# The experts' first product with its weights stationary and its tokens moving

## The reference, cut to what matters

```
t = rmsnorm(layernorm(h), norm_scale)
g = t @ gate_w.T + gate_b                       # 16 experts
top_vals, top_idx = top_k(g, 4); route_w = softmax(top_vals)
h1 = einsum('nh,ech->nec', t, mlp1_w) + mlp1_b  # per expert 192 -> 768
a  = min(glu, 7) * sigmoid(1.702 * min(glu, 7)) * (clip(lin, -7, 7) + 1)
y  = einsum('nec,ehc->neh', a, mlp2_w) + mlp2_b # per expert 384 -> 192
out = x + sum over experts of comb[n, e] * y[n, e]
```

## Time and profile before

| | |
|---|---|
| median of 3 runs | 792.63 us (792.56 to 793.79) |
| the profiled execution | 790.85 us, its span 789.1 us |
| PE busy | 695.0 us (88% of the span), 4250 instructions |
| PEld (weight loads) | 416.3 us (53%) |
| DVE, ACT, POOL busy | 434.6 (55%), 389.8 (49%), 347.8 us (44%) |
| mean granted clock of TensorE | 0.942 of full speed |
| DMA | 76.60 MB, mean 97 GB/s |

### The profile page before, as it was taken

How to read it: one execution, slowest core, us unless ns; L and a number is a source line. 1 busy time by engine, 2 the same in 40 slices (tenths; PEclk the granted TensorE clock), 3 DMA queues, 4 the chain that set the end, 5 groups by cost and what they waited for, 6 DMA issues and landing times.

```text
span 789.1 us, 15394 instructions
## 1 busy us (share of the span) xinstructions
PE 695.0 (88%) x4250; PEld 416.3 (53%) x4251; DVE 434.6 (55%) x1275; ACT 389.8 (49%) x784; POOL 347.8 (44%) x403
## 2 busy tenths in 40 slices
PE   4588989788867999999999995699999999999990
PEld 4557786578632222222222223377777777777760
DVE  0153757675672577777666644355555555555540
ACT  0032436533313999899989891134434344343430
POOL 4121223222230255555555444156666666666661
PEclk9798999999995999999999996599999999999995
DMA  9999980000014122322222200233323333233324
GB/s 275 411 389 320 321 274 1 1 1 1 21 55 108 61 55 104 98 91 100 63 82 103 103 24 22 79 68 52 52 43 51 52 52 52 43 51 52 52 31 70
DMA packets 31140, 76.60 MB, mean 97 GB/s; under 512 B 4335, under 2 KB 24672, under 8 KB 28672
## 3 DMA queue, kind: packets, MB, share of 16 engines
q1 hardware_dynamic: 17156, 59.50, 24.1%
q0 software_dynamic: 12400, 15.50, 9.8%
q10 hardware_dynamic: 1552, 1.18, 0.5%
HBM read 59.49 MB, written 40.11 MB: 126 GB/s over the span
## 4 chain that ended last, share of the span: by engine, by line
PE 72%; DVE 9%; DMA 4%; POOL 4%; ACT 4%; issue 3%; SPq 1%; ACTq 0%; DVEq 0%; POOLq 0%
PE ps L815 13%; PE ps L946 11%; PE ps L947 11%; PE ps L802 9%; PE ps L965 8%; PE ps L656 3%; DMA big<-patches 3%; PE ps L956 3%; ACT mid L1073 2%; POOL rstd L443 2%; PE ps L732 1%; DVE stat L1165 1%; DVE mid L1173 1%; PE ps L742 1%; PE ps L629 1%
## 5 line engine op out<-in xcount | busy, mean ns | idle before, releaser
L1073 ACT ACTIVATE mid<-ps 128x1536 f32<-128x1536 f32 x144 | 200.1, 1457 | 27.1 <-PE ps L802 27.1
L815 PE MATMUL ps<-mid 128*32 128x384 f32 x1152 | 123.6, 502 | 3.4 <-POOL mid L491 2.0
L566 POOL TENSOR_TENSOR mid<-mid 128x384 f32<-128x384 f32 x63 | 62.5, 991 | 99.8 <-PE ps L956 78.0
L946 PE MATMUL ps<-big,mid 128*128 x252 | 104.6, 497 | 0.3 <-issue 0.3
L947 PE MATMUL ps<-big,mid 65*128 x252 | 104.0, 493 | 0.0
L802 PE MATMUL ps<-mid 52*128 52x512 f16 x432 | 88.3, 389 | 6.2 <-ACT mid L1073 5.6
L965 PEld LDWEIGHTS ps<-big,mid 128*128 128x128 f32 x378 | 64.6, 189 | 18.4 <-issue 2.0
L965 PE MATMUL ps<-big,mid 128*128 x378 | 71.9, 326 | 1.5 <-DVE mid L1509 1.5
L1501 DVE TENSOR_SCALAR mid<-ps 128x384 f32<-128x384 f32 x63 | 35.1, 558 | 68.6 <-PE ps L947 68.6
L517 POOL DMA_INDIRECT expert_in<-t_row,slot_u x48 | 47.9, 999 | 46.0 <-DVE slot_u L1391 35.0
L1115 ACT ACTIVATE mid<-ps,mid 128x192 f32<-128x192 f32 x63 | 26.6, 422 | 84.3 <-PE ps L965 81.4
(11 more groups left out here) (224 smaller groups left out, 1192.7 us busy)
## 6 DMA issues: line engine op xcount, KB each, us to landing
expert_in<-expert_in SPq DMA_DIRECT2D x16, 1358.5 KB, 36.4
mid<-expert_in SPq DMA_DIRECT2D x63, 104.5 KB, 2.1
big<-patches SPq DMA_DIRECT2D x3, 2048.0 KB, 32.0
big<-w_a SPq DMA_DIRECT2D x4, 1536.0 KB
big<-w SPq DMA_DIRECT2D x4, 1152.0 KB
big<-w_b SPq DMA_DIRECT2D x4, 780.0 KB
big<-patches SPq DMA_DIRECT2D x4, 512.0 KB, 7.5
expert_in<-zero_rows POOLq DMA_DIRECT2D x1, 1567.5 KB, 16.2
```

The costliest lines, as they stand in the source:

```text
L566: nc.gpsimd.tensor_tensor(actv[r], prod[r], sig[r], ALU.mult).then_inc(actv_ready, 1)
L815: last = nc.tensor.matmul(oacc[32 * g:32 * g + 32, 0:QW], vhead[par][:, kb, :], probs[kb % 3][:, g * QW:(g + 1) * QW], start=(kb == 0), st ...
L946: nc.tensor.matmul(o, xtT[r][:, 0:P], w1a_sb[:, bass.ds(ex * 768 + half * FF, FF)], start=True, stop=False)
L1073: nc.scalar.activation(probs[kb % 3], SETS[kb % 2], ACT.Exp, scale=0.5).then_inc(probs_ready, 1)
```

## The change

The first weights are no longer kept in SBUF. SP fetches them for every tile, four tiles deep (NW = 4): `w1_t[q]` (128 rows by 768) and, as two transfers, `w1_h[q]`, in which rows 128 to 191 of the glu half lie at partitions 0 to 63 and those of the lin half at partitions 64 to 127. In the product the weights are stationary, in pieces of 128 columns, and the 128 transposed tokens move. The result is then already transposed (expert channels on partitions), so `act_transpose` and `actT_copy` are gone, and `mlp2` takes `actv` as it is. The products with 64 rows use the two row groups of the array through `tile_position`; for that, channels 128 to 191 of each token must lie on both partition halves, so `t_row` carries them twice (RW = 273) and the second token transpose is full. The bias is a column per expert and piece, `b1_cols`, made once: a transfer of 96 rows of 128, a transpose on TensorE before the first head, and two DVE operations. DVE adds it in `clip`, in pieces of 128 columns; the +1 of lin is in its bias. SP issues the weights of tiles 0 and 1 after `plan_ready` and ahead of its wait for `rows_out`. `mlp2` has two banks, 5 and 6. ACT's `sigmoid` and `y_tile` and POOL's `expert` and `add_rows` do the same work as before.

```diff
-COMB = C
-TOKEN = C + E
-RW = C + E + 1
+COMB = C + CB
+TOKEN = COMB + E
+RW = TOKEN + 1
+NW = 4
+HROW = P // 2
...
-        w1a_sb = big[:, 0:E * 768]
-        w1b_sb = big[:, E * 768:2 * E * 768]
-        w2_sb = big[:, 2 * E * 768:]
+        at[0] = 0
+        v_perm = carve(NT * C).rearrange("p (t c) -> p t c", t=NT)
+        w2_sb = carve(E * 3 * C)
+        w1_t = [carve(768) for _ in range(NW)]
+        w1_h = [carve(FF) for _ in range(NW)]
+        b1_rows = carve(P)[0:E * 6]
+        b1_cols = carve(E * 6)
+        t_row = carve(RW)
...
+            sp.wait_ge(v_in, 16 * NB)
+            sp.dma_start(b1_rows, w1_b[CB:CB + 1, :].rearrange("o (k c) -> (o k) c", c=P)).then_inc(b1_in, 16)
             for e in range(0, E, 4):
-                loads += [(w1b_sb[0:CB + 1, e * 768:(e + 4) * 768], w1_b[:, e * 768:(e + 4) * 768]),
-                          (w2_sb[:, e * 3 * C:(e + 4) * 3 * C], w2[:, e * 3 * C:(e + 4) * 3 * C]),
-                          (w1a_sb[:, e * 768:(e + 4) * 768], w1_a[:, e * 768:(e + 4) * 768])]
...
+                sp.wait_ge(vhead_ready, e // 4 + 1)
+                sp.dma_start(w2_sb[:, e * 3 * C:(e + 4) * 3 * C], w2[:, e * 3 * C:(e + 4) * 3 * C]).then_inc(w_in, 16)
...
+            def load_weights(j, q):
+
+                if not isinstance(j, int) or j >= NW:
+                    sp.wait_ge(h_done, j * 2 - (2 * NW - 2))
+                ex = sp.value_load(ej_i[0:1, bass.ds(j, 1)], min_val=0, max_val=E - 1)
+                sp.dma_start(w1_t[q], w1_a[:, bass.ds(ex * 768, 768)]).then_inc(w1_in[q], 16)
+                for half in range(2):
+                    sp.dma_start(w1_h[q][HROW * half:HROW * half + CB, :],
+                                 w1_b[0:CB, bass.ds(ex * 768 + half * FF, FF)]).then_inc(w1_in[q], 16)
...
+            load_weights(0, 0)
+            load_weights(1, 1)
+            sp.wait_ge(rows_out, 16 * (TOPK * NT + 1))
+            load_rows(0, 0)
+            load_rows(1, 1)
...
+            with sp.Fori(1, MT // NW) as i:
+                for q in range(NW):
+                    load_weights(i * NW + q, q)
+                    load_rows(i * NW + q, q % 2)
...
-                    pool.wait_ge(aT_psum, j - 1)
+                    pool.wait_ge(y_psum, j - 1)
...
+            pe.wait_ge(b1_in, 16)
+            nc.tensor.transpose(b7[:, 0:E * 6], b1_rows, ident[0:E * 6, 0:E * 6]).then_inc(b1_psum, 1)
             pe_head(0, None, 0, True, False)
...
-                nc.tensor.transpose(o[0:CB, P:2 * P], xt[r][:, P:C], ident[:]).then_inc(x_read, 1)
+                nc.tensor.transpose(o[:, P:2 * P], xt[r][:, P:2 * P], ident[:]).then_inc(x_read, 1)
+
+            def mlp1(j, q, n_loaded):
+
+                r = q % 2
+                pe.wait_ge(xT_ready, j + 1)
+                pe.wait_ge(w1_in[q], n_loaded)
+                if not isinstance(j, int) or j >= 2:
+                    pe.wait_ge(lin_ready, j - 1)
+                banks = [bank(1 + 2 * half + r) for half in range(2)]
+                for half in range(2):
+                    for c in range(3):
+                        nc.tensor.matmul(banks[half][:, c * P:(c + 1) * P], w1_t[q][:, half * FF + c * P:half * FF + (c + 1) * P],
+                                         xtT[r][:, 0:P], start=(c == 0), stop=False)
+                for c in range(3):
+                    for half in range(2):
+                        rows_ = slice(HROW * half, HROW * half + CB)
+                        last = nc.tensor.matmul(banks[half][:, c * P:(c + 1) * P], w1_h[q][rows_, c * P:(c + 1) * P],
+                                                xtT[r][rows_, P:2 * P], start=False, stop=(c == 2),
+                                                tile_position=(HROW * half, 0))
+                        if c == 2:
+                            last.then_inc(h_done, 1)
...
                 pe.wait_ge(actv_ready, j + 1)
+                if not isinstance(j, int) or j >= 2:
+                    pe.wait_ge(y_sb, j - 1)
                 for c in range(3):
...
+                    last = nc.tensor.matmul(bank(5 + r)[:, 0:C], actv[r][:, c * P:(c + 1) * P],
...
+            def tile_work(j, q, loaded):
+
+                if not isinstance(j, int) or j + 1 < MT:
+                    x_transpose(j + 1, (q + 1) % 2, loaded * 2 + 16 * ((q + 1) // 2 + 1))
+                mlp1(j, q, loaded * 3 + 48)
+                if not isinstance(j, int) or j >= 2:
+                    mlp2(j - 2, q % 2)
...
-                nc.scalar.activation(xtT[r][:, 0:P], o[:, 0:P], ACT.Identity)
-                nc.scalar.activation(xtT[r][0:CB, P:2 * P], o[0:CB, P:2 * P], ACT.Identity).then_inc(xT_ready, 1)
+                nc.scalar.activation(xtT[r], o[:, 0:2 * P], ACT.Identity).then_inc(xT_ready, 1)
...
+                nc.vector.scalar_tensor_tensor(t_row[:, C:C + CB], ln[:, P:C], rms[:], nscale_sb[:, P:C], ALU.mult, ALU.mult)
...
+                ex = dve.value_load(ej_i[0:1, bass.ds(j, 1)], min_val=0, max_val=E - 1)
...
+                for c in range(3):
+                    last = nc.vector.tensor_scalar(glu[r][:, c * P:(c + 1) * P], bank(1 + r)[:, c * P:(c + 1) * P],
+                                                   b1_cols[:, bass.ds(ex * 6 + c, 1)], 7.0, ALU.add, ALU.min)
+                last.then_inc(glu_ready, 1)
...
+                for c in range(3):
+                    last = nc.vector.tensor_scalar(lin[r][:, c * P:(c + 1) * P], bank(3 + r)[:, c * P:(c + 1) * P],
+                                                   b1_cols[:, bass.ds(ex * 6 + (3 + c), 1)], 8.0, ALU.add, ALU.min)
+                last.then_inc(lin_ready, 1)
```

139 lines of the change are left out of this document (37 added, 102 removed).

## The result

The changed kernel takes **788.69 us** (median of 4 runs, 788.33 to 788.94) against 793.21 us before (4 runs beside them): ratio 0.9942, 95% interval 0.9925 to 0.9959. So it is faster by 0.6%, some 4.5 us, where I had forecast 770. The profiled execution has a span of 787.1 us.

The account below looks back on a forecast made before the run. TensorE was taken to bound the expert stage: 4.11 to 3.67 us a tile, counted 62 times, gives -27.3 us. With +4.6 once per run, the profiled 790.85 became 768.2; placed 1.8 below the median, this gave 770 us, range 755 to 804.

Parts of the forecast that it names:

- SyncE at 3.5 us a tile: Expert stage: SyncE's work per tile with the added weight transfers, 3.5 us, just under TensorE's 3.67; bounds 3.3 and 3.9.
- a fuller queue: SyncE in the expert stage: a transfer's issue might rise from 0.34 to 0.45 us, making 3.9 us a tile.
- rival (B): Expert stage: SyncE is the bound at 3.9 us a tile, 784 us in all; chance 0.15.
- TensorE's side: Expert stage: TensorE's work per tile falls from 4.11 to 3.67 us and sets the tile, -27.3 us.
- The borders: First product on TensorE: entering and leaving the row-tiled part costs 0.46 us a tile; lower bound nothing.
- Rival (A): First product: the row groups do not overlap, half part 1.34 us, tile 4.34 us, 811 us in all; chance 0.24.
- DMA bytes: Expert stage: the DMA engines need 2.85 us a tile, below 3.67, a share of 0.78.
- Rival (C): Expert stage: scattered rows land later, POOL and ACT wait, tile 4.0 us, 790 us in all; chance 0.07.
- the opening's larger zero rows: Opening transfer: zero rows grow by 31%, 480 KB, costing +1.2 us; bounds 0 and 3.0.
- The bias wait: Before the attention: TensorE's transpose of b1 waits for its transfer, delaying L815 by 2.7 us; bounds 1.5 and 3.5.
- SyncE's start: After the plan: SyncE issues six weight transfers before the first token rows, +1.7 us; bounds 0 and 3.
- The tail: End of the last tile: no activation transposes and no copy of them, -1.0 us.

Follow-up runs that it names:

- e18_before: The kernel before, unchanged, profiled once more: 792.97 us.
- e19_after: The changed kernel, unchanged, profiled once more: 789.23 us.
- e1_fixed: The changed kernel with first-product weights fetched for the first four tiles only and reused by all later tiles: 766.49 us.
- e6_serial: Against e1_fixed, both 64-row halves of the first product set on row group 0, reading the first half's weights: 806.48 us.

## Why the prediction failed

By the second pair of profiles (e18_before and e19_after; both with long heads), the difference is made up so, all from first or last starts of instructions. Each is one execution, and the parts ahead of the plan vary by 1 to 3 us between executions of one program:

| part | forecast | measured |
|---|---|---|
| first weighted sum (L815, L834) | +3.9 | 249.67 to 253.33: +3.7 |
| from there to the plan | 0 | 250.2 to 249.4: -0.7 |
| plan to first product | +1.7 | 7.3 to 10.3: +3.0 |
| first product to the last second product's start | -27.3 | 263.4 to 251.8: -11.6 |
| from there to the end | -1.0 | 20.7 to 22.6: +1.9 |
| span | -22.7 | 791.2 to 787.5: -3.7 |

**The step that failed: SyncE at 3.5 us a tile.** The sum was 1.39 for the work it had, 1.23 for three transfers with what lies around them, 0.57 for a register load and 0.3 for gaps. Measured are 1.58 instead of 1.23 for the three transfers, of which 0.29 is the two to 64 partitions at 0.480 instead of 0.337 us; 0.95 instead of 0.87 for the load and its gaps; and 1.33 instead of 1.39 for the row transfer with its load. The turn of the loop, on no row of mine, adds some 0.3 us every fourth round. So its mean round is 3.93 us, above TensorE's 3.60 to 3.67, and the tile goes by SyncE. I had 3.9 as a bound, but hung it on a fuller queue; the run with narrow transfers shows the same 480 ns at half the DMA share, and the run cut by columns shows that the form of the transfer decides. This is rival (B), with SyncE as the bound and nearly its price, though not for the reason that it gave: it put the loop at -13.0, and the two pairs of profiles give -13.3 and -11.6. I gave it 0.15 although my two sums lay 0.17 us apart: a price read from transfers of one shape was used for another. The part of the miss that the form makes, 12.7 of 18.7 us, is shown by a run; the rest, down to the 770 us that were forecast, is what merging the transfers then gave (772.0).

**TensorE's side was right.** Forecast 3.67 us, measured 3.60: full part 1.43 for 1.34, half part 0.87 for 0.67 and a border, second product 1.08 for 0.98, token transposes 0.22. The borders cost 0.39 together where I took 0.46. Rival (A) is out: the run on one row group shows what it would have been without fetches, 806.5 us. The Trainium skill (TensorEngine Tiling (Array Packing), Key Properties) says that different tiles can load weights and multiply in parallel, and the two runs agree for float32 loads of 128 columns (3.60 against 4.26 us); it says that a change of tiling mode drains the array, and the 0.19 to 0.20 us at the border, on one row group too, are compatible with that; a weight load that nothing hides could make the same, and no run here tells the two apart. Without SyncE's limit the forecast holds: 766.5 us without fetches, 772.0 with one transfer, for 770.

**DMA bytes: a small term.** Forecast a share of 0.78, measured 0.87. Rival (C) is real once SyncE is out of the way, with waits of ACT and POOL on scattered rows, and is worth up to 5.5 us (7.6 in the stage). In the changed kernel these waits are all but absent, as every engine has time. What the opening's larger zero rows cost can't be told from the profiles: v's load (L364 before, L369 after) was issued at 246.5 us before and 246.1 after in the first pair, but at 245.9 and 247.0 in the second, and over all eighteen profiles with the larger rows between 244.2 and 247.0. The +1.2 of the forecast is neither shown nor refuted.

**The bias wait was right in kind and size.** From v's load to the first weighted sum it took 3.6 and 3.8 us in the two profiles of the kernel before, 6.4 and 6.3 in those of the changed one: 2.8 and 2.5 more, for a forecast of 2.7. (The table's +3.7 holds 1.1 us of a later opening as well.) I had not counted that TensorE's clock can come up later: in the window from 255 to 260 us it was granted 0.50 (1.2 GHz) in the changed kernel, behind the 5.23 us of waiting, and 1.00 in the kernel before. The second pair has 0.77 and 0.94 there and no loss (-0.7 from the first weighted sum to the plan); the first pair has one, 246.4 us before and 250.4 after, of which the longer heads are 1.7. That the wait makes the clock late is not shown: the run with narrow transfers has the same wait, ends it 1.2 us sooner, and was granted 1.00 in this window.

```profile
255.00:260.00 5.00, 5.00 (x26) 0.74 (x30) 0.00 (x0) 3.10 (x3) 0.00 (x0) 0.50 0.47 193
```

**SyncE's start was undersized.** Two weight blocks were taken at 2.1 us each from right behind the plan. They came 2.95 us apart (504.04, 506.99), and the first one 1.19 us behind the plan: 3.0 us in place of 1.7, again the price of SyncE's work.

**The tail has the wrong sign.** I took off the transposes and their copy. But the two halves of the first product now finish together: the last L976 ends at 760.20, and only then can VectorE do all its seven operations, so POOL's product starts at 762.74, 2.5 us later; before, one half was clipped beside the other's product, and it was 1.3 us (763.33 to 764.66). Behind that product POOL scatters the rows of tile 60, the third from the end (764.20), and the last tile's result is copied into the same buffer only when they have landed (ACT at 767.74, for the scatter at 769.02):

```profile
762.74 0.99 POOL L585 TENSOR_TENSOR mid<-mid 128x384 f32<-128x384 f32 x1 [0.55 <-DVE mid L1516]
764.20 1.58 POOL L592 DMA_INDIRECT out<-mid  x1 [0.47 <-issue]
766.08 1.56 POOL L592 DMA_INDIRECT odd_sum<-mid  x1 [0.30 <-issue]
769.02 1.55 POOL L592 DMA_INDIRECT out<-mid  x1 [1.37 <-ACT mid L1117]
```

Before, the last three scatters stood about as close (766.38, 768.26, 771.31), so the gain of TensorE's shorter end is hidden behind that chain, which now starts 4.0 us behind the end of the last first product (760.20 to 764.20) where it started 3.1 behind (763.33 to 766.38). This reading is from the profile alone; no run changed it.

**A version that beats both** came out of the study: one weight transfer a tile, the bias transpose inside the first head, and the first rows ahead of the second tile's weights. It took 769.44 us on one chip (ratio 0.9700) and 772.80 on another (0.9761), 2.4 to 3.0% below the kernel before. Keeping all first weights in SBUF, with the expert's address given to each weight load, was not tried.

## What to carry to other kernels

Before an engine that only issues transfers is called free, sum its round as carefully as TensorE's: here three register-addressed transfers and a register load a tile took 2.5 us (1.58 and 0.95), and merging them into one array gave back some 15.5 us without moving a byte less, most of it because the merged transfer goes to 128 partitions. Price a transfer by rows of its own shape, partitions included, count the turn of the loop, and where two engines' sums lie closer than the worst price in them, give the other engine the chance that this implies. When two halves of a product are made to finish together, what consumes them loses its overlap. And before a small difference between two profiles is explained, profile the same kernel twice: eight runs had touched on a difference that the unchanged kernel shows as well.

## What the runs showed of the hardware

- SyncE's time to issue a register-addressed load of the weights did not depend on its bytes: 0.337 us to 128 partitions, 0.480 to 64, whether a tile's weights are 590 KB or 49 KB (0.336 and 0.480 in the run with narrow transfers); the same bytes cut into 128-partition pieces cost 0.333 each. Transfers with a fixed address to 65 partitions cost 0.330 (L374 of the kernel before), so few partitions alone do not make it dear.
- Float32 weight loads and products of 128 columns in two row groups run side by side: twelve instructions in 0.87 us against 1.53 on one row group (e1_fixed and e6_serial).
- The attention of one and the same kernel differs from one profile to another: over eleven intervals 205.9 or 208.5 us in the two profiles of the kernel before, 207.6 or 208.7 in those of the changed one. In the changed kernel's first profile, in the first head of TensorE's loop, the copy of the transposed stacks starts 1.2 us behind the last recorded transpose (296.98 to 298.15), where it is 0.03 in the first profile of the kernel before (292.30 to 292.33). The cause was not found.
